# Scan layers: the norms' factors split by VectorE instead of GpSimd, and another order of the work in a slot

## The reference

```python
h = _layernorm(x, n1_g, n1_b)                     # first norm
p = h @ w_in + b_in                               # 96 -> 192
local = depthwise_conv_3x3(p, k_conv)             # 9 taps
lr, rl, tb, bt = ema_scan(local, 4 directions)    # y = 0.6 * y_prev + 0.4 * local
mixed = 0.25 * (lr + rl + tb + bt) + local
mixed = _layernorm(mixed, on_g, on_b)             # second norm, of the scanned item
x = x + (mixed @ w_out + b_out)
h2 = _layernorm(x, n2_g, n2_b)                    # third norm
m = gelu(h2 @ w1 + b1) @ w2 + b2                  # 96 -> 384 -> 96
return x + m
```

## Time and profile before

| | us |
|---|---|
| median of three runs | 3670.02 (3669.94 to 3678.01) |
| the profiled execution | 3670.32 |
| its span, first to last instruction | 3668.7 |
| scan layers in it | from 3166 to the end, some 500 |
| TensorE busy in the span | 3141.9 (86%) |
| VectorE busy | 2582.0 (70%) |
| ScalarE busy | 1821.7 (50%) |
| GpSimd busy | 583.8 (16%) |

### The profile page before, as it was taken

How to read it: one execution, slowest core, us unless ns; L and a number is a source line. 1 busy time by engine, 2 the same in 40 slices (tenths; PEclk the granted TensorE clock), 3 DMA queues, 4 the chain that set the end, 5 groups by cost and what they waited for, 6 DMA issues and landing times. The chain is left out here.

```text
span 3668.7 us, 136690 instructions
## 1 busy us (share of the span) xinstructions
PE 3141.9 (86%) x50394; PEld 2339.4 (64%) x50394; DVE 2582.0 (70%) x12076; ACT 1821.7 (50%) x5594; POOL 583.8 (16%) x2420
## 2 busy tenths in 40 slices
PE   5378999999958947999999999999999998577787
PEld 1134666566622315888988888889888887254454
DVE  4567999999974635777777777777777778466562
ACT  2215999999933025444544444444444445133342
POOL 0001111111100001222222222222222222111110
PEclk9678999999978966555555555555555555678888
DMA  1312333333330000000000000000000000000000
GB/s 32 108 47 95 108 107 107 107 107 107 108 91 1 10 7 2 5 5 5 5 5 5 5 5 5 5 5 5 5 5 5 5 5 4 11 1 1 0 5 13
DMA packets 54608, 116.12 MB, mean 32 GB/s; under 512 B 12313, under 2 KB 19801, under 8 KB 53692
## 3 DMA queue, kind: packets, MB, share of 16 engines
q1 hardware_dynamic: 37104, 53.42, 5.3%
q0 software_dynamic: 13824, 50.34, 3.9%
q10 hardware_dynamic: 2956, 3.15, 0.4%
HBM read 84.06 MB, written 22.81 MB: 29 GB/s over the span
## 5 line engine op out<-in xcount | busy, mean ns | idle before, releaser
L504 PE MATMUL g_zr<-g_hp,g_wp 97*128 97x4 f16 x24576 | 1082.6, 171 | 53.4 <-issue 49.0
L504 PEld LDWEIGHTS g_zr<-g_hp,g_wp 97*128 97x128 f16 x24576 | 956.4, 108 | 157.4 <-issue 51.3
L595 ACT ACTIVATE g_e<-g_tn 96x8 f32<-96x8 f32 x2048 | 437.0, 213 | 557.8 <-DVE g_tn L540 557.8
L480 PE MATMUL g_zr<-s_inner,g_wi 96*128 (+2 forms) x6240 | 585.1, 234 | 61.9 <-issue 39.7
L612 POOL COPY s_y<-g_hs 96x8 f32 x2048 | 401.0, 196 | 1374.9 <-DVE g_hs L555 1374.9
L553 DVE TENSOR_TENSOR_SCAN g_hp<-g_gates,g_e 96x16 f16<-96x16 f32 x2048 | 382.1, 187 | 316.7 <-ACT g_e L595 207.6
L592 ACT ACTIVATE g_gates<-g_zr 96x16 f32<-96x16 f32 x2048 | 399.5, 195 | 315.5 <-PE g_zr L504 315.4
L511 PE MATMUL g_n<-g_hp,g_wp 97*128 97x8 f16 x8192 | 520.1, 174 | 0.0
L844 DVE CUSTOM_DVE_ANT_0 a_negated<-a_scores,a_mask 128x1024 f32<-128x1024 f32 x384 | 468.0, 1219 | 59.1 <-PE a_scores L762 41.2
L870 ACT ACTIVATE a_probs<-a_negated,a_negmax 128x1024 f32<-128x1024 f32 x384 | 442.4, 1152 | 26.1 <-DVE a_negmax L844 16.3
L540 DVE TENSOR_TENSOR_SCAN g_tn<-g_gates,g_n 96x24 f32<-96x24 f32 x2048 | 387.8, 189 | 95.7 <-ACT g_gates L592 95.7
(11 more groups left out here) (324 smaller groups left out, 3058.5 us busy)
## 6 DMA issues: line engine op xcount, KB each, us to landing
a_mask<-in_L_mask POOLq DMA_DIRECT2D x96, 512.0 KB, 5.6
a_k<-k_rows SPq DMA_DIRECT2D x96, 144.0 KB
q_rows<-r_q_parts SPq DMA_DIRECT2D x12, 576.0 KB, 7.4
k_rows<-r_k_parts SPq DMA_DIRECT2D x12, 576.0 KB, 7.4
a_q<-q_rows SPq DMA_DIRECT2D x96, 72.0 KB
o_parts<-a_o_sb SPq DMA_DIRECT2D x384, 18.0 KB
o_part<-o_parts SPq DMA_DIRECT2D x32, 192.0 KB
out_x<-x SPq DMA_DIRECT2D x4, 384.0 KB, 3.0
```

The costliest lines, as they stand in the source:

```text
L480: pe.matmul(o, wi[0:K, half, pw, d * NG + g, :], x, start=first, stop=False, skip_group_check=True)
L504: mm = pe.matmul(zr_bank[u, k][:, 1 - g, d, :, at], wp[0:97, part, (2 * u + d) * NG + g, :], hp[u][0:97, d * NB:(d + 1) * NB, e], start=False,
L595: act.activation(e1[u][:, :, 0], tn[u][:, :, 2], ACT.Tanh, scale=to_tanh).then_inc(n_and_zh[u], 1)
```

## The change

What it does:

- GpSimd's `split` is gone. The same four steps stand on VectorE in `invert`, behind the reciprocal, each waiting for the one before.
- The second norm's root, reciprocal and split for item e come at the end of slot k instead of the head of slot k + 1. On VectorE they stand ahead of the down-projection's add-back.
- The second norm's spread stands ahead of transposes 0 and 1, and its first half waits for the first half of the down-projection's add-back alone.
- The first norm's variance waits for the first half of the out-projection's add-back alone.
- The third norm's squares, variance and root move from behind the in-projection to directly behind those of the first norm (variance between transposes 2, 3 and 4, 5, into `ring1`); its reciprocal and split follow the first norm's on VectorE, ahead of the first norm's product. Its spread stands ahead of mix tile 0 instead of behind it.
- The taps are spread otherwise: 0 behind the second norm's products, 1, then 2 and 3 between the two centrings, 4 to 8 behind the third norm's product (before: 0; 1; 2; 3, 4; 5; 6 to 8).

```diff
-            def split(parts, inv, inverted, i, done):
-                po.wait_ge(inverted, i + 1)
-                po.tensor_copy(parts[:, :], inv[:, :]).then_inc(done, 1)
...
-            def invert(to, dev, rooted, count, done):
-                ve.wait_ge(rooted, count)
-                ve.reciprocal(to[:, :], dev[:, :]).then_inc(done, 1)
+            def invert(inv, dev, parts, rooted, i, inverted, done):
+                ve.wait_ge(rooted, i + 1)
+                ve.reciprocal(inv[:, :], dev[:, :]).then_inc(inverted, 1)
+                ve.wait_ge(inverted, i + 1)
+                ve.tensor_scalar(parts[:, :], inv[:, :], 1.0, None, ALU.mult).then_inc(done, 1)
+                ve.wait_ge(done, 4 * i + 1)
+                ve.tensor_tensor(inv[64:128, :], inv[64:128, :], parts[64:128, :], ALU.subtract).then_inc(done, 1)
+                ve.wait_ge(done, 4 * i + 2)
+                ve.tensor_scalar(parts[64:128, :], inv[64:128, :], 1.0, None, ALU.mult).then_inc(done, 1)
+                ve.wait_ge(done, 4 * i + 3)
+                ve.tensor_tensor(parts[96:128, :], inv[96:128, :], parts[96:128, :], ALU.subtract).then_inc(done, 1)
```

TensorE's part of a slot (waits first, then what is issued):

```diff
-                if k >= 3 and m is not None:
-                    pe.wait_ge(e_rooted, m + 1)
+                if m is not None:
+                    pe.wait_ge(e_split, 4 * (m + 1))
+                    for h in range(2):
+                        if m >= 1:
+                            pe.wait_ge(m_added, 2 * m + h - 1)
+                        elif f is not None:
+                            pe.wait_ge(padded, 4 * f)
+                        spread_half(ring[h], h, e_parts, e_spread)
                 if e is not None:
                     pe.wait_ge(tapped, 2 * TAPS * (e + 1))
                     turn_pairs(e, range(0, 2))
-                if k >= 4 and m is not None:
-                    pe.wait_ge(m_added, 2 * (k - 3))
-                elif f is not None and f:
-                    pe.wait_ge(padded, 4 * f)
...
                     elif m is not None:
-                        pe.wait_ge(e_added, 2 * (m + 1))
+                        pe.wait_ge(e_added, 2 * m + 1)
...
                     variance(ring[0], collect[C], f_squares, f_var)
                 if e is not None:
-                    turn_pairs(e, range(2, 6))
+                    turn_pairs(e, range(2, 4))
+                if m is not None:
+                    pe.wait_ge(m_squared, m + 1)
+                    if g is not None:
+                        pe.wait_ge(unloaded, 2 * (g - NB + 1))
+                    variance(ring[1], collect[C], m_squares, m_var)
+                if e is not None:
+                    turn_pairs(e, range(4, 6))
                 if f is not None:
                     pe.wait_ge(f_split, 4 * (f + 1))
                     for h in range(2):
+                        if h and m is not None:
+                            pe.wait_ge(m_rooted, m + 1)
                         spread_half(ring[h], h, f_parts, f_spread)
                     project_in(f, 0)
...
                 if m is not None:
-                    pe.wait_ge(m_squared, m + 1)
-                    if f is not None:
-                        pe.wait_ge(padded, 4 * (f + 1))
-                    elif g is not None:
-                        pe.wait_ge(unloaded, 2 * (g - NB + 1))
-                    variance(ring[0], collect[C], m_squares, m_var)
+                    pe.wait_ge(m_split, 4 * (m + 1))
+                    for h in range(2):
+                        if f is not None:
+                            pe.wait_ge(padded, 4 * f + 3 + h)
+                        spread_half(ring[h], h, m_parts, m_spread)
...
                     mix_tile(0)
                 if m is not None:
-                    pe.wait_ge(m_split, 4 * (m + 1))
-                    for h in range(2):
-                        spread_half(ring[h], h, m_parts, m_spread)
                     project_up(m, range(0, 2))
```

VectorE's and ScalarE's calls in a slot, only those that move:

```diff
-                if m is not None:
-                    invert(e_inv, e_dev, e_rooted, m + 1, e_inverted)
...
                 if f is not None:
-                    invert(f_inv, f_dev, f_rooted, f + 1, f_inverted)
-                if v is not None:
-                    taps(v, 2, 3)
+                    invert(f_inv, f_dev, f_parts, f_rooted, f, f_inverted, f_split)
+                if m is not None:
+                    invert(m_inv, m_dev, m_parts, m_rooted, m, m_inverted, m_split)
...
                 if v is not None:
-                    taps(v, 3, 5)
+                    taps(v, 2, 4)
                 if e is not None:
                     centre_tokens(e, 1)
-                if m is not None:
-                    invert(m_inv, m_dev, m_rooted, m + 1, m_inverted)
-                if v is not None:
-                    taps(v, 5, 6)
...
                 if v is not None:
-                    taps(v, 6, 9)
+                    taps(v, 4, 9)
+                if e is not None:
+                    invert(e_inv, e_dev, e_parts, e_rooted, e, e_inverted, e_split)
                 if m is not None:
                     add_back(down_ready, m, 1, m_added)
```

More of the change, by code:

```diff
@@ L1493, in _ @@
                     po.memset(strip, 0.0).then_inc(edges, 1)
-            def split(parts, inv, inverted, i, done):
-                po.wait_ge(inverted, i + 1)
-                po.tensor_copy(parts[:, :], inv[:, :]).then_inc(done, 1)
[L1499 to L1504, removed]
             for k in slots:
                 f, v, e, m, g = stages(k)
-                if m is not None:
-                    split(e_parts, e_inv, e_inverted, m, e_split)
-                if f is not None:
-                    split(f_parts, f_inv, f_inverted, f, f_split)
-                if m is not None:
-                    split(m_parts, m_inv, m_inverted, m, m_split)
                 if e is not None:
@@ L1623, in _ @@
                     elif m is not None:
-                        pe.wait_ge(e_added, 2 * (m + 1))
+                        pe.wait_ge(e_added, 2 * m + 1)
+                    elif f:
+                        pe.wait_ge(padded, 4 * f)
                     variance(ring[0], collect[C], f_squares, f_var)
                 if e is not None:
-                    turn_pairs(e, range(2, 6))
+                    turn_pairs(e, range(2, 4))
[6 more added lines that the diff above has]
+                    turn_pairs(e, range(4, 6))
                 if f is not None:
@@ L1669, in _ @@
                         mm.then_inc(down_ready, 1)
+                if e is not None:
+                    pe.wait_ge(e_rooted, e + 1)
         @block.scalar
@@ L1707, in _ @@
                 f, v, e, m, g = stages(k)
-                if m is not None:
-                    root(e_dev, turn[1], e_var, m + 1, e_rooted)
                 if f is not None:
@@ L1723, in _ @@
                         act.activation(x[:, part(g, h)], ring[h][0:C, :], ACT.Copy).then_inc(unloaded, 1)
+                if m is not None:
+                    act.wait_ge(e_added, 2 * (m + 1))
+                    act.activation(m_squares[:, :], res[0:C, own(m)], ACT.Square).then_inc(m_squared, 1)
                 if f is not None:
@@ L1728, in _ @@
                 if m is not None:
-                    act.wait_ge(e_added, 2 * (m + 1))
-                    act.activation(m_squares[:, :], res[0:C, own(m)], ACT.Square).then_inc(m_squared, 1)
+                    root(m_dev, ring[1], m_var, m + 1, m_rooted)
                 if e is not None:
@@ L1740, in _ @@
                     take_in(f, 1)
-                if m is not None:
-                    root(m_dev, ring[0], m_var, m + 1, m_rooted)
                 if e is not None:
@@ L1750, in _ @@
                     gelu(m, range(2, 6))
+                if e is not None:
+                    root(e_dev, turn[1], e_var, e + 1, e_rooted)
         @block.vector
@@ L1786, in _ @@
                 if m is not None:
-                    invert(e_inv, e_dev, e_rooted, m + 1, e_inverted)
+                    for h in range(2):
+                        ve.wait_ge(e_spread, 2 * m + h + 1)
+                        ve.wait_ge(e_copied, 2 * (m + 1))
+                        for s in range(2):
+                            ve.tensor_tensor(e_xn[:, s, bank(h)], e_xn[:, s, bank(h)], ring[h][0:C, :],
+                                             ALU.mult).then_inc(e_normed, 1)
                 if v is not None:
@@ L1793, in _ @@
                 if m is not None:
[L1794 to L1799, removed]
                     add_back(out_ready, m, 0, e_added)
```

4 lines of the change are left out of this document (removed).

## The result

| | before | changed |
|---|---|---|
| median, us | 3669.98 (3667.72 to 3678.01, four runs) | 3606.6 (3603.52 to 3612.03, four runs) |
| profiled execution, us | 3670.32 | 3612.03 |
| its span | 3668.7 | 3610.4 |

What follows compares the result with a forecast made beforehand. Neither engine being full, the dependency chain was taken as the bound, with TensorE's low clock after gaps. 3670.3 us less 42 (five full slots) less 12 (other slots) gave 3616 us, range 3608 to 3628, or 3600 to 3642 with two rivals.

Steps and rivals of the forecast that it cites:

- The split: The four split steps on VectorE take 1.0 us together, against 3.4 on GpSimd beside VectorE's taps.
- Opening -3.8: Full slot, end of down-projection to start of out-projection: 2.2 us instead of 5.96.
- out-projection -2.8: Full slot: the out-projection runs at the high clock level, 3.69 us instead of 6.48.
- P to in-projection: From P, the out-projection's end, the in-projection starts at P + 8.05 us instead of 9.32: -1.3.
- Mix tile 0 at P + 17.05, set by VectorE: Mix tile 0 starts 17.05 us after the out-projection's end (P) instead of 19.8, released by VectorE's tokens.
- The toll, +2.0 a slot: TensorE waits before mix tile 0, which then runs at low clock: 2.8 us in some seven slots of ten.
- 42 were forecast: Gain over five full slots, out-projection of slot 3 to that of slot 8: 8.5 us a slot.
- The other slots, 12 forecast: Slots outside the five full ones gain 12 us together.
- Openings of slots 0 to 3: Quicker splits gain 0.7 us in slot 0, nothing in 1, 2.4 in 2, 1.4 in slot 3's opening.
- Slot 8: Mix tile 0 behind the third norm's invert costs 2.5 us, opening and out-projection give some 5.5: net 3.
- Slot 9: Mix tile 0 starts at 12.6 instead of 10.3 us, costing 1.2; net gain 4.
- the one without toll: Rival: low clock falls into the in-projection, where VectorE is awaited anyway; 10 us less, 3606; chance 0.12.

Runs made afterwards that it cites:

- e3: Changed kernel with the scanned item's root, reciprocal and split put back at the head of the next slot; 3643.73 us, ratio 0.9924 to the kernel before.
- e2: Kernel before, order kept, only the split moved to VectorE behind each reciprocal; 3652.84 us, ratio 0.9954.
- e6: Kernel before plus 12 matmuls nobody reads between transposes 0 and 1 and the wait for the scanned item's split; 3651.45 us, ratio 0.9956.
- e4: Changed kernel with the third norm's squares, variance, root, reciprocal, split and spread put back where they stood before; 3610.91 us, ratio 0.9838 to the kernel before.
- e10: Changed kernel run once more, unaltered, on the chip of e9; 3603.35 us, ratio 0.9813 to the kernel before.
- e5: Changed kernel plus matmuls nobody reads (fillers) behind the first norm's spread and ahead of mix tile 0; 3600.63 us, ratio 0.9823 to the kernel before.
- e9: Changed kernel with the fillers of e5 and the third norm's split on GpSimd in slots 3 to 7 only; 3596.22 us, ratio 0.9796 to the kernel before.
- e7: Changed kernel with the third norm's split alone back on GpSimd; 3607.15 us, ratio 0.9843 to the kernel before.

## Why the prediction was right

**The split.** Forecast 1.0 us. The forms of the changed kernel:

```profile
L1763 DVE TENSOR_SCALAR e_m_parts<-e_m_inv 128x128 bf16<-128x128 f32 x5 | 1.1, 226 | 0.2
...
L1765 DVE TENSOR_TENSOR e_m_inv<-e_m_inv,e_m_parts 64x128 f32<-64x128 f32 x5 | 1.4, 290 | 0.2
...
L1767 DVE TENSOR_SCALAR e_m_parts<-e_m_inv 64x128 bf16<-64x128 f32 x5 | 1.1, 224 | 0.2
...
L1769 DVE TENSOR_TENSOR e_m_parts<-e_m_inv,e_m_parts 32x128 bf16<-32x128 f32 x5 | 1.4, 289 | 0.2
```

0.226 + 0.290 + 0.224 + 0.289 = 1.03. The two rows of 128 columns from the setup were the right ones, and the width in partitions does not matter: 32 partitions take as long as 64. By the cycle table of the Trainium skill (VectorE: DVE Perf Modes, on the TRN2 errata) it would have been 0.64, as an estimate; the measurement decides.

**Opening -3.8 and out-projection -2.8:** measured -3.9 and -2.8. Of the first, e3 takes 2.6 away again; the quicker split is 0.5 (e2: 5.5 us instead of 5.96), and 0.9 lies between e2 and e3, in which tap 0 stands behind the product. Of the second, e3 takes all away, and e6 gives it alone in four slots of seven. **P to in-projection:** forecast P + 8.05, measured 8.1; e4 shows why it is not 6.5.

**Mix tile 0 at P + 17.05, set by VectorE.** Right in slots 3 and 4, where it came at 16.9. In slot 4 the tile waits for the tokens:

```profile
3317.07 1.96 PE L1539 MATMUL e_mix<-e_along_rows,e_tokens 128*96 128x128 f32 x16 [1.43 <-DVE e_tokens L1775]
```

In slots 5 to 7 it came at 17.7 behind the last pad and spread (3409.30, 3410.05 above), while the second tokens instruction had ended at 3409.5:

```profile
3407.76 1.75 DVE L1775 SCALAR_TENSOR_TENSOR e_tokens<-e_sums,e_tokens 128x1536 f32<-128x1536 f32 x1
```

**The toll, +2.0 a slot.** Its place was wrong, its size nearly right. The prediction had the low level begin while TensorE waits for the tokens, with the in-projection at the high level. The windows of slot 4 to 5 and of slot 6:

```profile
3311.90:3352.70 40.80, 35.70 (x237) 24.56 (x235) 33.11 (x44) 20.45 (x52) 3.22 (x1) 1.00 0.00 1
...
3400.60:3414.10 13.50, 12.90 (x42) 7.86 (x43) 13.00 (x13) 4.06 (x12) 0.00 (x0) 0.50 0.01 1
```

The level falls near the start of the in-projection (at about 3400.5), whose work it makes slow, and lasts into mix tile 0, which takes 3.47 + 2.79 = 6.3 instead of 4.65. In slots 3 and 4 it lasts 3.4 us and is over within the in-projection. So the cost is 2.5 us in three slots of five and none in two: 1.5 a slot in this execution, not 2.0. Five slots gave 46.8 us where 42 were forecast. I had put it at seven slots in ten; with e10 it is four in ten.

The cause is shown best where the executions agree. In slots 8 and 9 mix tile 0 takes 6.5 to 7.5 us in both profiles of the changed kernel and 4.65 in e5 and e9, with fillers. In the full slots e5 alone would prove little, since e10 had four of 45.1 us without any filler: in its slots 5 and 6 the low level came as well, but was over ahead of mix tile 0.

**The other slots, 12 forecast.** Openings of slots 0 to 3: 4.5 forecast, 2.2 measured (4.2, of which 2.0 had come before the scan layers began). What I left out is in the chain ahead of slot 3's out-projection:

```profile
3237.76 3.76 POOL e_e_squares L1499
...
3245.81 3.73 PE e_mix L1573 x4
...
3249.54 0.44 PE e_ring L1519 x4
```

GpSimd's sum of squares took 3.76, beside VectorE's taps which now lie there (2.35 before), and then the centring of the next item, at the low level, holds the spread until 3249.5. Slot 8: 3 forecast, 4.1 measured. Slot 9: 4 forecast, 1.4 measured; its mix tile 0 ran at the low level, 3.70 + 3.77, where I had put 4.65. Sum: 2.0 + 2.2 + 46.8 + 4.1 + 1.4 + 1.8 (slots 10 and 11) = 58.3.

So the trace shows 58.3 where 54 were forecast, and the sum is closer than its terms: 4.8 more in the full slots, 2.0 ahead of the scan layers, where the change touches nothing, and 2.5 less in the other slots. The other 5 us between forecast and median are the difference between the profiled execution and the median of the four. The median is in the range of 3600 to 3642, but just under the forecast's own 3608 to 3628, in which only the profiled execution lies. Of the rivals, the one without toll (3606) gave the median; by its own mechanism it held in two slots of five here, and in four of five in e10.

## What to carry to other kernels

Where short steps on several engines pass one value around, look for the place in each engine's queue where its inputs are ready and the engine is idle; moving one such group ahead of a wait (here under the down-projection) gave some 36 of 63 us, while the quicker engine for the same steps gave nothing that could be measured once the order was right. Charge a gap of TensorE twice: for itself, and for the matmuls behind it that run at 1.2 GHz (here 6.5 us instead of 3.7 for the out-projection). Before moving a second group, count what it now stands in front of: the third norm's factor gained behind the in-projection what it cost ahead of it, and in slot 8 it only cost. And before a few us are put down to an edit, profile the same kernel twice.

## What was not expected of the hardware

GpSimd's time for one split ranged from 1.65 us, with VectorE waiting or in a reciprocal, over 3.4 beside taps, to 6.9 beside tokens and taps, where its last step on 32 partitions alone took 2.48 instead of 0.42. VectorE paid too: in e7 four taps took 5.10 instead of 4.86 and the tokens 1.98 instead of 1.75.

The same program has several times: the low level of the clock fell in other slots from one execution to the next, and its four runs are 8.5 us apart. The mean granted clock of each run goes with it: 0.703, 0.703, 0.705 and 0.706 at 3612.03, 3607.18, 3606.01 and 3603.52 us, and in e4, e9 and e10 too no faster run has the lower one. How much of the spread the clock makes is open all the same: another part lies ahead of the scan layers, only one run in each set is profiled, and no run here holds the clock fixed.
